# Four-stage gated attention and expert network: column maxima over partitions moved from GpSimd to TensorE and VectorE, context sums spread

## What is computed

```python
x = x + tanh(g_xattn[0]) * xattn0(layernorm(x), ctx)     # linear attention, 16 heads, gate
x = x + tanh(g_ffn[0])   * ffn0(layernorm(x))            # 512 -> 2048 -> 512, gelu
x = x + tanh(g_xattn[1]) * xattn1(layernorm(x), ctx)     # softmax over 64 context rows
x = x + tanh(g_ffn[1])   * experts(layernorm(x))         # 8 groups, top 8 of 32, silu
# xattn0: q = phi(y Wq), k = phi(ctx Wk), v = ctx Wv, gate = sigmoid(y Wg + bg)
#         out = ((q (k^T v)) / (q sum k)) * gate @ Wo
```

## Time and profile before

| | |
|---|---|
| median of three runs | 1888.39 us (1887.68 to 1888.73) |
| the profiled execution | 1887.19 us, span 1885.4 us |
| PE busy | 1846.4 us (98%) |
| DVE, ACT, POOL busy | 995.9, 538.6, 323.5 us (53%, 29%, 17%) |

### The profile page before, as it was taken

The page is one execution under the profiler, slowest core; times in us unless marked ns, Lnnn a source line. Parts: engine busy times, 40 slices in busy tenths (PEclk is TensorE's granted clock), DMA queues, the critical chain, the costliest instruction groups (busy, mean ns, idle before and its releaser), DMA issues.

```text
span 1885.4 us, 24612 instructions
## 1 busy us (share of the span) xinstructions
PE 1846.4 (98%) x9552; PEld 905.6 (48%) x9552; DVE 995.9 (53%) x2036; ACT 538.6 (29%) x801; POOL 323.5 (17%) x299
## 2 busy tenths in 40 slices
PE   8799999999999999999999999999999999999999
PEld 3445554644444444444444444444444444444444
DVE  5676776754554455454436554545445455554422
ACT  3224433312221122122112233233333223333321
POOL 1123322222021120202010011111111111111111
PEclk9899999999999999999999999999999999999999
DMA  5124433333414223340310200101010101000000
GB/s 159 55 62 129 140 118 95 96 129 65 104 42 127 90 68 104 70 125 27 90 54 9 76 1 23 32 1 54 1 54 1 54 1 54 1 23 1 1 23 23
DMA packets 135830, 112.10 MB, mean 59 GB/s; under 512 B 75554, under 2 KB 92066, under 8 KB 135714
## 3 DMA queue, kind: packets, MB, share of 16 engines
q1 hardware_dynamic: 135714, 110.53, 19.7%
HBM read 78.00 MB, written 32.51 MB: 59 GB/s over the span
## 4 chain that ended last, share of the span: by engine, by line
PE 83%; issue 9%; DVE 3%; POOL 2%; DMA 2%; ACT 1%; POOLq 0%; SPq 0%; DVEq 0%; ACTq 0%
PE bank L923 44%; PE bank L1012 17%; PE bank L1092 10%; PE bank L992 4%; PE bank L932 3%; PE bank L977 1%; POOL arena L897 1%; PE bank L958 1%; PE bank L1079 1%; PE bank L1027 1%; POOL arena L871 0%; PE bank L1054 0%; DVE arena L1278 0%; DMA arena<-in_L_xattn_Wkv 0%; DMA arena<-x_after_ffn 0%
## 5 line engine op out<-in xcount | busy, mean ns | idle before, releaser
L923 PE MATMUL bank<-arena 128*128 128x512 f16 x4608 | 1042.2, 380 | 8.4 <-DVE arena L1299 7.3
L923 PEld LDWEIGHTS bank<-arena 128*128 128x128 f16 x4608 | 451.1, 98 | 538.9 <-DVE arena L1299 7.8
L1012 PE MATMUL bank<-arena 128*128 128x512 f16 x1536 | 352.1, 379 | 1.2 <-DVE arena L1506 1.2
L1092 PE MATMUL bank<-arena 128*128 128x512 f16 x1152 | 264.3, 379 | 0.9 <-POOL arena L897 0.9
L1648 DVE SCALAR_TENSOR_TENSOR arena<-bank,arena 128x512 f32<-128x512 f32 x96 | 72.0, 750 | 329.0 <-PE bank L923 329.0
L1191 ACT ACTIVATE arena<-bank,arena 128x512 f32<-128x512 f32 x128 | 99.5, 778 | 493.5 <-PE bank L923 490.5
L1012 PEld LDWEIGHTS bank<-arena 128*128 128x128 f16 x1536 | 150.1, 98 | 181.1 <-DVE arena L1506 1.7
L897 POOL TENSOR_TENSOR arena<-arena 128x512 f16<-128x512 f32 x96 | 111.0, 1157 | 626.0 <-ACT arena L1228 626.0
L1504 DVE TENSOR_SCALAR arena<-arena 128x512 f16<-128x512 f32 x128 | 65.8, 514 | 281.6 <-ACT arena L1191 281.3
L1092 PEld LDWEIGHTS bank<-arena 128*128 128x128 f16 x1152 | 112.0, 98 | 128.4 <-POOL arena L897 1.4
L1506 DVE SCALAR_TENSOR_TENSOR arena<-arena 128x512 f16<-128x512 f32 x128 | 118.0, 922 | 4.6
(11 more groups left out here) (159 smaller groups left out, 1215.8 us busy)
## 6 DMA issues: line engine op xcount, KB each, us to landing
arena<-in_L_ffn_proj SPq DMA_DIRECT2D x64, 256.0 KB, 2.9
arena<-in_L_ffn_gate_up_proj SPq DMA_DIRECT2D x96, 96.0 KB, 2.0
x_after_attention<-arena SPq DMA_DIRECT2D x8, 1024.0 KB, 5.2
arena<-x_after_attention SPq DMA_DIRECT2D x8, 1024.0 KB, 5.6
x_after_ffn<-arena SPq DMA_DIRECT2D x8, 1024.0 KB, 4.3
arena<-x_after_ffn SPq DMA_DIRECT2D x8, 1024.0 KB, 6.2
arena<-in_x SPq DMA_DIRECT2D x7, 1024.0 KB, 5.5
normalised_blocks<-arena SPq DMA_DIRECT2D x28, 256.0 KB, 2.0
```

The costliest lines, as they stand in the source:

```text
L923: m = e.matmul(bank[b][:, :], wT[l][:, c, tile * P:(tile + 1) * P], y[h][:, c, :], start=n == 0, stop=n == NPASS - 1)
L1012: m = e.matmul(bank[t][:, :], hv[h][:, 0, t * P:(t + 1) * P], w2T[l][:, j, :], start=j == 0 and i == 0, stop=j == NH - 1 and i == 2)
L1092: m = e.matmul(bank[t][:, :], hv[h][:, 0, t * P:(t + 1) * P], dnT[l][:, j, :], start=j == 0 and i == 0, stop=j == NR - 1 and i == 2)
```

## The change

GpSimd's `partition_all_reduce` goes. A new pair of steps takes its place for each of the twelve maxima. In `allt` TensorE turns the column of 128 values into a row of one PSUM bank, and VectorE takes the maximum of that row into one cell. In `allb` TensorE multiplies that cell with a row of ones, which spreads it over 128 partitions, and VectorE copies the column out of PSUM. In the pump, `allt` comes at the flush after `all`, `allb` at the flush after that, and `pow` at the next. The context sums `kvsum` stand between the `q` and `gate` projections of block 0, `numden` of block 0 between its gates, and `turn` of block 1 behind them. `tables`, b1 and c go into the `out` steps of b = 1. The splits of weight o no longer lie in front of block 1.

```diff
                 if t == SIZE[name] - 1:
                     add("all", name)
-                    late.append(lambda: after_max(name))
+                    late.append(lambda: over_partitions(name))
...
+    def over(kind, name):
+        add(kind, name, banks=1)
+
+    def over_partitions(name):
+        over("allt", name)
+        late.append(lambda: (over("allb", name), late.append(lambda: after_max(name))))
...
     add("kvv", 0, banks=1)
+    over("allt", "q")
     norm(2)
     add("kvv", 1, banks=1)
+    over("allb", "q")
     add("keysv", 0)
     add("pow", "q")
...
     add("kvv", 3, banks=1)
+    over("allt", "g")
     add("keysv", 2)
...
+    norms = ln_tasks(("A", 1), apart=True)
     for j in range(NC):
         add("q", 0, j, banks=1)
         if j == 0:
             add("keysv", 3)
+            over("allb", "g")
             add("pow", "g")
             split("g")
+            add("vmax")
+            add("all", "v")
+        else:
+            add("kvsum", j - 1, banks=4)
+        if j == 1:
+            over("allt", "v")
+        if j == 2:
+            over("allb", "v")
         flush()
+        if j == 2:
+            add("consts")
+            add("pow", "v")
+        if j > 1:
+            norm(2)
     scaled.update("qg")
-    add("consts")
     add("xload", "A", 2)
-    norms = ln_tasks(("A", 1), apart=True)
     for j in range(NC):
         add("gate", 0, j, banks=1)
-        norm()
         if j == 0:
-            add("vmax")
-            add("all", "v")
-        if j == 2:
-            add("pow", "v")
+            add("kvsum", 3, banks=4)
+        else:
+            add("numden", 0, j - 1, banks=2)
+        if j < 2:
+            norm()
         weights(N_O)
-    for t in range(4):
-        add("kvsum", t, banks=4)
-        if t < 2:
-            norm()
-    for t in range(NT):
-        norm()
-        add("numden", 0, t, banks=2)
-        weights(N_O)
-    add("tables")
-    add("all", "b1")
-    add("ctxmax")
-    add("all", "c")
-    late.append(lambda: add("pow", "c"))
+    norm()
+    add("numden", 0, NT - 1, banks=2)
+    norm(3)
+    weights(N_O)
+    weights(N_O)
...
             add("out", b - 1, t, banks=1)
+            if b == 1 and t == 0:
+                add("tables")
+                add("all", "b1")
+                add("ctxmax")
+                add("all", "c")
+            if b == 1 and t in (1, 2):
+                over("allt" if t == 1 else "allb", "b1")
+                over("allt" if t == 1 else "allb", "c")
+            if b == 1 and t == 3:
+                add("pow", "c")
...
-            elif kind == "all":
-                ap = sc["m" + step[1]]
-                w.wait_ge(all_in, n)
-                e.partition_all_reduce(ap, ap, P, bass.bass_isa.ReduceOp.max).then_inc(all_out)
...
+            elif kind == "allt":
+                k = bank_free(step)
+                w.wait_ge(const, C_ID)
+                w.wait_ge(all_in, nth["all", step[1]])
+                e.transpose(bank[k][0:1, 0:P], sc["m" + step[1]], ident).then_inc(all_turned)
+            elif kind == "allb":
+                k = bank_free(step)
+                w.wait_ge(const, C_ALL)
+                w.wait_ge(all_row, nth["allt", step[1]])
+                e.matmul(bank[k][:, 0:1], onesP[0:1, :], row[step[1]][0:1, :], start=True, stop=True).then_inc(all_spread)
...
+            elif kind == "allt":
+                w.wait_ge(all_turned, n)
+                e.tensor_reduce(row[step[1]][0:1, :], bank[bank_of[step, 0]][0:1, 0:P], AX.X, ALU.max).then_inc(all_row)
+            elif kind == "allb":
+                w.wait_ge(all_spread, n)
+                e.tensor_copy(sc["m" + step[1]], bank[bank_of[step, 0]][:, 0:1]).then_inc(all_out)
```

More of the change, by code:

```diff
@@ L517, in build @@
     wmax = small(64)
+    row = {n: small(1) for n in ("c", "v", "b1", *SIZE)}
     gains, tanhg = small(4), small(4)
@@ L577, in build @@
     w_mx, w_hi, w_lo = sem("w_mx"), sem("w_hi"), sem("w_lo")
-    s_chain, all_in, all_out, half_in, half_out = (sem(n) for n in ("s_chain", "all_in", "all_out", "half_in", "half_out"))
+    s_chain, all_in, all_turned, all_row, all_spread, all_out, half_in, half_out = (
+        sem(n) for n in ("s_chain", "all_in", "all_turned", "all_row", "all_spread", "all_out", "half_in", "half_out"))
     scale_of = {n: sem(f"scale_{n}") for n in ("c", "v", *SIZE)}
@@ L618, in freed @@
             return g_tanh, n
+        if kind == "allt":
+            return all_row, n
+        if kind == "allb":
+            return all_out, n
         if kind == "kvk":
@@ L1318, in vector_program @@
                 e.tensor_reduce(sc["m" + name], wmax[:, c], AX.X, ALU.max).then_inc(all_in)
+            elif kind == "allt":
[4 more added lines that the diff above has]
+                e.tensor_copy(sc["m" + step[1]], bank[bank_of[step, 0]][:, 0:1]).then_inc(all_out)
             elif kind == "pow":
                 name = step[1]
-                w.wait_ge(all_out, nth["all", name])
+                w.wait_ge(all_out, nth["allb", name])
                 if name == "v":
@@ L1354, in vector_program @@
                 if name == "1":
-                    w.wait_ge(all_out, nth["all", "b1"])
+                    w.wait_ge(all_out, nth["allb", "b1"])
                     e.tensor_scalar(o, o, NORM2 * D, TINY, ALU.mult, ALU.max).then_inc(s_chain)
```

## The result

The changed kernel takes 1926.41 us (1925.75 to 1928.41) where the kernel before takes 1888.25: the ratio is 1.0203 [1.019, 1.0216]. Its profiled execution has a span of 1923.9 us, against 1885.4 before: +38.5. A slowdown was forecast, of 31.5 us to 1920; the places were nearly all the forecast ones, but not every price.

A forecast was written before the change was run, and what follows sets the result against it. TensorE was taken as the bound, with waits behind GpSimd's maxima. Terms from -3.1 to +10.5 summed to +31.5 us on 1887.19, 1918.7, given as 1920 us; main case 1904 to 1934, with two rivals 1896 to 1935.

The forecast's parts named there:

- (a): Up to `q` of block 1: old sum waits go, nearly as many new ones come; start 89.4, not 92.51: -3.1 us.
- (b): To block 2's first `turn`: VectorE waits four times 3.0 us for loads; +7.3, and +0.8 for the clock's fall.
- (c): `tables`, b1 and c behind the first `out`: VectorE has no slack there, TensorE waits; +3.5 us (0 to 5.1).
- (d): Weights 1 and 2: `allt` and `allb` adjacent on TensorE, row maximum behind a `numden` eviction; +1.8 us each.
- (e): Weight 1's splits to weight 2's maxima, b = 4: load waits delay the turn; +7.8, and +2.2 for the clock.
- (f): The old stall at 293, a wait for a normalised input behind GpSimd, goes: -7.1 us in the sum.
- (g): Second stage: waits for row maxima behind evictions, 3 x 3.5 and 2.6 for gw; clock falls +3.4 us.
- the main case: The whole kernel is slowed by the summed terms, with either clock: 1904 to 1934 us, 75%.
- the rival of a full fall each time: Second stage: the clock falls in full after each pause, 4 x 2.6 instead of 3.4 us, 1927; 20%.
- That the new waits are covered: Whole kernel: VectorE finishes `all` and row maximum before TensorE reaches the step; only old pauses count, 1860 us; 9%.
- That the loads don't hold VectorE: In (b) and (e): SyncE issues loads earlier, both terms and the old pause at 118 go; 1897 us, 10%.
- That the change doesn't do what it says: Rival on whether the maxima really leave GpSimd; its size and chance are not stated in the text given.

The follow-up runs named there:

- The first experiment: The changed kernel with the pump in step: from weight 1 on, no tile is measured ahead of the splits; 1901.94 us, 1.0073 of the kernel before.
- fourth experiment: The changed kernel with tables and the maxima of b1 and c ahead of block 1's `q` again; 1925.51 us, 1.0194 of the kernel before.
- the second experiment: The changed kernel with `allt` and `allb` three flushes later each in the second stage, pump in step there too; 1908.41 us, 1.0113 of the kernel before.
- the kernel in the old order without them: All repairs, maxima on TensorE, but context sums, block 0's `numden`, first norms and weight o's splits placed as in the kernel before; 1871.99 us, 0.9918 of it.
- two smaller repairs: Two separate edits of the changed kernel: g's turn and spreading behind the first projections, 1924.47 us; tables, b1 and c ahead of block 1's `q`, 1925.51 us.
- the third experiment: The changed kernel with g's turn behind the first projection of `q` and its spreading behind the second; 1924.47 us, 1.0197 of the kernel before.
- the two kernels with GpSimd's maxima: The changed kernel's order with GpSimd taking the maxima at the place of the turn: 1908.61 us; the same with the pump in step: 1894.68 us.
- fifth experiment: The changed kernel with pump in step, all pairs apart, g's pair, tables and block 1's last turns moved; 1868.33 us, 0.9892 of the kernel before.

## Why the prediction was right

An offset below is the start of a piece of TensorE's work in after less its start in before. Each comes of one profiled execution. The first forty matmuls alone, ahead of every difference, take 19.28 us in before and 20.30 in after, and 19.1 to 20.4 over all ten traces, so about 1 us of any offset can be chance.

What a fall of the clock costs was charged from the earlier trace rows: 1.7 us (0.35 of 4.9) behind the 4.0 us of idling at 118, 2.6 (half of 5.2) behind the 4.3 at 293. In after the twelve matmuls behind a fall took 4.19 us at 46, 4.23 at 90, 4.19 at 128, 4.54 at 260, and 4.11, 5.30 and 4.45 in the second stage, 1.4 to 2.6 more than the usual 2.75.

**(a) To `q` of block 1.** Forecast -3.1 at its start, measured -2.0 there and -3.0 at the end of its twelve matmuls, which took 4.23 us where they took 5.30. The pause in front of the first `q` was put at some 4 us and is 3.86; the fall behind it shows as 4.19 us for twelve matmuls, 1.4 more than the usual 2.75; 2.5 had been charged. That the end meets the forecast is partly luck. The first `q` starts at 46.25 instead of 45.0, mostly by those forty matmuls, the fall costs less, and VectorE's serial tail takes 7.3 us (83.2 to 90.5), where the prediction put 6.3 to 6.5. The items that it lists come to 7.6 if each of the two evictions of `numden` takes its 1.35, so that sum was a slip.

**(b) To block 2's `turn`.** +8.3 from the end of that `q`, forecast +7.3. The four waits for loads were put at 12.0 and measure 12.6. The other half microsecond and more is `wlo` 8, which takes 1.76 us instead of the 0.74 that is usual. The first experiment shows the cause of the waits: with the loads free of the splits they disappear, and the pause with them. `wlo` 8 takes 1.75 us there too, so its length is another matter. The fall of the clock behind it cost 0.2 more than the old one, not 0.8.

**(c) Tables.** +3.1 at `q` of block 2, forecast +3.5; the wait for c is 1.92 us, put at 2.1. The size came out, but not all of the mechanism: the wait for the last turn, by which the forecast got to 3.5, is not there. The rest is mostly the two turns and two spreading products of b1 and c themselves, about 1.0 us. Taking the tables away was not worth the 3.1 (fourth experiment): a later start and a deeper fall of the clock behind the loads used it up.

**(d) The pairs of weights 1 and 2.** Forecast 1.8 each. The pause is 1.70 us at 176 and again at 306, and the stretches lose 2.45 and 2.3 us. The rest is the pair itself and what stands around it: the second experiment puts a covered pair at 0.42 us. The prediction charged the wait alone.

**(e) The turn in b = 4.** +10.3 against +7.8, the largest miss in the first part. The three waits ahead of `norm` are 4.38, 2.71 and 2.73 us in the timeline of VectorE, 0.8 more than three of 3.0; the `wlo` ahead of them takes 1.74, 1.0 more than usual; 0.7 stays unexplained. The clock behind it cost 2.3, forecast 2.2.

**(f) The stall at 293.** The sum has -7.1 for it: 4.3 for the wait, 2.6 for the clock and 0.2 on the `turn` behind. What keeps GpSimd's `half` back for 7.10 us, the cause behind this term, no run shows; they show that the wait is not there in after, where no maximum is left on GpSimd. Block 6's first `q` starts there at 318.41 without a bracket, and its twelve matmuls take 2.75 us where they took 5.30. The offset falls from +25.4 to +18.45 us at their end: -6.9, and by 0.3 more with the `turn` behind it.

**A gain not seen.** At the `turn` behind block 3's gates 0.7 us come back (+11.0 to +10.25): a small old pause of 0.61 us there, not in the sum.

**(g) The second stage.** +20.2 us, forecast 16.5. The pauses are nearly right: three of 0.48 + 2.55 and one of 0.77 + 1.42 make 11.3. From start to start, with the pairs and the ends of the matmuls ahead of them, the four stretches lose 14.5 us, where the sum had 13.1. The clock is the term that was too small by most: the twelve matmuls behind the three pauses took 4.11, 5.30 and 4.45 us instead of 2.75, 5.6 more in all, and 5.9 with the next ones, where I had charged 3.4 by taking half. The granted clock from 671 to 677 us was 0.50, the lowest that any window shows. Behind gw the timeline of TensorE in the kernel after shows no fall, with a granted clock of 1.00 from 933.8 to 937:

```profile
931.87 0.27 PE L982 MATMUL bank<-arena 128*1 128x128 f32 x1 [0.77 <-DVE arena L1355]
933.56 0.35 PE L987 MATMUL bank<-arena 1*128 1x1 f32 x2 [1.42 <-DVE arena L1358]
933.84 2.76 PE L1049 MATMUL bank<-arena 128*128 128x512 f16 x12
```

So the truth lay between the main case and the rival of a full fall each time (10.4); that the time of this rival, 1927, is nearly the one measured is chance, since other terms made up the rest. Three of these four pauses, 3.0 us of idling, were followed by a fall, the one of 2.2 was not; the prediction had charged all four alike.

Why the pause is 2.55 us is in VectorE's timeline of the kernel after: the row maximum (L1358) stands behind four evictions (L1557) of 2.72 us, as forecast from the earlier trace rows.

```profile
496.75 0.17 DVE L1355 TENSOR_REDUCE arena<-arena 128x1 f32<-128x12 f32 x1
496.83 2.72 DVE L1557 SCALAR_TENSOR_TENSOR arena<-bank,arena 128x512 f32<-128x512 f32 x4
499.47 0.27 DVE L1358 TENSOR_REDUCE arena<-bank 1x1 f32<-1x128 f32 x1
```

**The rivals.** That the new waits are covered falls with the list of waits; the repaired kernel shows it was a matter of places, since with the pairs apart the same instructions are nearly all covered, and 1868 is near the 1860 that this rival gave. That the loads don't hold VectorE falls with 31.2 us of such waits in after. That the change doesn't do what it says falls too: no maximum is left on GpSimd, and its list of waits in after has only 0.2 us, at the start, with nothing shown that it waits for.

**Sum.** The offsets above go from -3.0 to +18.3 at the second stage and +38.5 at the end, against +31.5: 3.7 us of the difference are the second stage, 2.5 of them its clock, and 2.5 are (e); the rest is small change of both signs, a microsecond each for (b) and the pairs of (d) among it.

## What to carry to other kernels

A step that waits for another engine belongs, in each engine's list, behind enough other work for its input to be there: with the same kinds of instructions, 58 us lay in the places of a few steps, above all in turn and spreading side by side around four evictions, and in tiles measured while their loads waited for the engine's own splits. When work moves from one engine to another, look first at what the old place delayed (here GpSimd's 6.75 to 7.82 us behind a maximum; the kernel in the old order without them was 16.6 us faster, the places of the pairs and the pump included), then at what queue the new place stands in. And repair the longest wait first: two smaller repairs ahead of it gave 2.8 us alone.

## What the runs showed of the hardware that was not expected

- The clock fell behind each of three pauses of 3.0 us in the second stage's dense work (twelve matmuls 4.11, 5.30, 4.45 us, usually 2.75; granted clock 0.50 from 671 to 677) and not behind one of 2.2 us (2.76; 1.00 from 933.8 to 937).
- The last pause alone doesn't tell whether it falls: behind the same wait of 1.92 us for c, twelve matmuls took 2.75 us in after (granted clock 1.00 from 139.8 to 142.5) and 3.46 in the third experiment (0.78 from 135.8 to 139.2). What made the difference was not found.
- GpSimd is idle on both sides of a partition maximum with nothing shown that it waits for: 5.76 to 6.39 us ahead, where it came from other work, and 6.75 to 7.82 behind, where no other engine held its next work, at a busy time of mostly 0.38 (before and the two kernels with GpSimd's maxima). Between two maxima in a row there is no such gap: in before the one of c starts at 99.61, 1.8 us after the one of b1 (97.42) ended, all of it a wait for VectorE, and in the two kernels with GpSimd's maxima it is 1.78, again for VectorE.
- A `wlo` of VectorE takes 0.74 us, and up to 1.76 where GpSimd's elementwise work on 128x512 runs beside it (in after at 103.07, with GpSimd busy from 103.01 to 105.84). In the first 440 us of the traces of before, after, the first and the fifth experiment every `wlo` with a row of its own that takes 1.0 us or more has such work beside it, and every one without it takes 0.72 to 0.75. No run separated the two on purpose.
